# Shared-kernel convolution with per-pixel selection: one block of constants, an earlier deviation, a shorter first selection and loads in another order

## The reference

```
logits = conv1x1(gn(x), coupler_w) + coupler_b
sel    = softmax(logits);  sel = sel / sel.sum()
conv   = conv3x3(gn(x), weight as 8*64 filters) + bias
out    = x + sum_s conv[s] * sel[s]
```

## Time and profile before

| what | value |
|---|---|
| median of three runs | 340.92 us (340.84 to 341.65) |
| the profiled execution | 341.6 us, span 339.8 us |
| PE busy | 324.7 us, 96% of the span |
| DVE busy | 277.7 us, 82% |
| POOL busy | 229.5 us, 68% |
| ACT busy | 109.2 us, 32% |
| DMA | 41.93 MB, mean 123 GB/s |

### The profile page before, as it was taken

The page is one execution under the profiler, slowest core; times in us unless marked ns, Lnnn a source line. Parts: engine busy times, 40 slices in busy tenths (PEclk is TensorE's granted clock), DMA queues, the critical chain, the costliest instruction groups (busy, mean ns, idle before and its releaser), DMA issues.

```text
span 339.8 us, 5413 instructions
## 1 busy us (share of the span) xinstructions
PE 324.7 (96%) x1684; PEld 152.7 (45%) x1684; DVE 277.7 (82%) x504; ACT 109.2 (32%) x159; POOL 229.5 (68%) x329
## 2 busy tenths in 40 slices
PE   8996999999998999999999999999999899999993
PEld 8433444445443444445444444444544344444441
DVE  2799899997799688887799688887799687777786
ACT  1688251176111162175221062175221011111110
POOL 3700788899984598899854599899854599434343
PEclk9999899999999999999999999999999999999999
DMA  6799399019940695019950595019820596011002
GB/s 214 292 265 215 76 215 224 7 41 243 244 115 0 168 214 119 3 42 237 206 154 3 152 218 128 0 35 236 179 49 0 146 221 134 0 38 31 3 1 69
DMA packets 30374, 41.93 MB, mean 123 GB/s; under 512 B 2128, under 2 KB 23248, under 8 KB 29968
## 3 DMA queue, kind: packets, MB, share of 16 engines
q1 hardware_dynamic: 29184, 37.78, 46.0%
q10 hardware_dynamic: 1168, 3.89, 3.9%
HBM read 12.56 MB, written 4.72 MB: 51 GB/s over the span
## 4 chain that ended last, share of the span: by engine, by line
PE 69%; DVE 19%; issue 4%; DMA 4%; POOL 2%; SPq 1%; ACT 1%; DVEq 1%; ACTq 0%
PE pair L398 42%; PE pair L410 14%; PE pair L406 10%; DVE high L823 4%; DVE pair L822 3%; DVE half L831 3%; DVE pair L806 2%; DVE pair L808 2%; DMA op<-v_tail 2%; DMA x_raw<-x 2%; POOL v_pts L1112 2%; PE side L388 1%; DVE mix L790 0%; DVE v_pts L996 0%; DVE top L780 0%
## 5 line engine op out<-in xcount | busy, mean ns | idle before, releaser
L398 PE MATMUL pair<-w_head,op 128*128 128x512 f16 x864 | 234.9, 381 | 6.8 <-DVE half L831 3.5
L398 PEld LDWEIGHTS pair<-w_head,op 128*128 128x128 f16 x864 | 83.5, 98 | 110.6 <-DVE half L831 8.5
L410 PE MATMUL pair<-w_tail,op 128*128 128x512 f16 x288 | 109.4, 380 | 0.0
L594 ACT ACTIVATE m_sb<-pair 128x512 f32<-128x512 f32 x72 | 42.9, 596 | 200.6 <-PE pair L410 194.0
L1135 POOL TENSOR_TENSOR quarter<-half 128x256 f32<-128x256 f32 x71 | 52.8, 744 | 65.9 <-DVE half L831 65.3
L822 DVE TENSOR_TENSOR pair<-pair,sel_now 128x512 f32<-128x512 f32 x71 | 49.4, 696 | 38.9 <-PE pair L410 38.9
L831 DVE TENSOR_TENSOR half<-pair,high 128x512 f32<-128x512 f32 x71 | 49.1, 692 | 10.2 <-DVE high L823 1.0
L406 PE MATMUL pair<-w_tail,op_two 128*128 128x512 f16 x144 | 54.9, 381 | 0.0
L806 DVE TENSOR_TENSOR pair<-pair,m_sb 128x512 f32<-128x512 f32 x72 | 49.6, 689 | 0.0
L808 DVE TENSOR_TENSOR pair<-m_sb,pair 128x512 f32<-128x512 f32 x72 | 49.3, 684 | 0.0
L823 DVE TENSOR_TENSOR high<-pair,sel_now 128x512 f32<-128x512 f32 x71 | 48.3, 680 | 0.0
(11 more groups left out here) (110 smaller groups left out, 197.4 us busy)
## 6 DMA issues: line engine op xcount, KB each, us to landing
op<-v_head SPq DMA_DIRECT2D x14, 600.0 KB, 8.0
x_res<-x_pix SPq DMA_DIRECT2D x8, 576.0 KB, 6.5
op_two<-v_head SPq DMA_DIRECT2D x14, 300.0 KB, 9.0
op<-v_tail SPq DMA_DIRECT2D x14, 300.0 KB, 6.8
op<-v_head SPq DMA_DIRECT2D x14, 288.0 KB, 8.4
out<-y_out SPq DMA_DIRECT2D x7, 576.0 KB, 4.0
x_raw<-x ACTq DMA_DIRECT2D x3, 1152.0 KB, 9.2
w_raw<-weight SPq DMA_DIRECT2D x3, 768.0 KB, 8.8
```

What stands on the lines that cost most here:

```text
L398: nc.tensor.matmul(dst, op[b][:, 0, j, at + r * PW:at + r * PW + P], w_head[:, j, r, :], start=fresh and r == 0, stop=False, skip_group_ch ...
L410: return nc.tensor.matmul(dst, op[b][:, 1, j, at:at + P], w_tail[:, j, 0, :], start=False, stop=True, skip_group_check=True)
L594: act.activation(m1_sb[:, i % LOOK, :], pair[i % SETS_OF_BANKS][:, 0, :], ACT.Copy).then_inc(m1_copied, 1)
```

## The change

**Constants.** `mats`, `coupler_w` (zeros included), `coupler_b` and bias become one block that the host lays out, `consts`, with one transfer on SP's queue in the place of `mats`. ACT's four transfers, POOL's memset and two semaphores go.

**Deviation.** On POOL `inverse_deviation(0)` stands ahead of all three pieces of the last x part, where one piece stood ahead of it.

**Coupler.** The two heads of the coupler weights move from DVE to ACT (`coupler_heads`, behind `first_heads(3, 0)`); DVE keeps the two tails.

**Weight tails.** `second_point_tails` has two instructions for three.

**Selection.** `divide_again`, the sum and the scaling of the first 12 columns become `weights_soon`, one instruction that scales and divides together. `divide_again(0, 0)` and the sum (`sums_soon`) follow in round 0 behind `halve(0)`. POOL's bias steps wait for them (`prep`).

**Order.** On DVE `seed(0, 0)` goes ahead of `mixed_tails`, both `last_row_tail` follow it, and `seed(1, 0)` goes ahead of `add_up(0, 0)` in one piece. SP's `load_res(0, 0)` goes behind `first_fill(0, 1)`. ACT's `load_ahead(1)` goes behind `copy_m1(1, 0)`. `combine` goes from DVE's tile 4 to tile 3, in all rounds that prepare a next one.

```diff
+        consts = sb("consts", [P, 3 * P + 2 * SETS + SETS + C])
...
-            sp.dma_start(mats[:, :, :], matrices).then_inc(mats_loaded, 16)
+            sp.dma_start(consts[:, :], constants).then_inc(consts_loaded, 16)
...
             first_fill(0, 0)
-            load_res(0, 0)
             first_fill(1, 0)
             first_fill(0, 1)
+            load_res(0, 0)
             first_fill(1, 1)
...
+            def coupler_heads():
+
+                act.activation(cw_pts[:, 0, 1:3, :], cw_pair.unsqueeze(1).to_broadcast([P, 2, 2 * SETS]), ACT.Copy,
+                               scale=half_scale[:, 1:2]).then_inc(c_heads, 1)
+                act.activation(cw_pts[:, 0, 0, :], cw_pair, ACT.Copy, scale=minus_half_scale[:, 1:2]).then_inc(c_heads, 1)
...
-            act.dma_start(bias_all[:, :], bias.partition_broadcast(P)).then_inc(small_loaded, 16)
-            act.dma_start(cb_all[:, :], coupler_b.partition_broadcast(P)).then_inc(small_loaded, 16)
-            act.wait_ge(cleared, 1)
-            for b in range(2):
-                act.dma_start(cw_pair[C * b:C * b + C, b, :], coupler_w).then_inc(small_loaded, 16)
...
                 w_heads_of(0, slice(r, r + 1))
-            load_ahead(1)
             first_heads(3, 0)
+            coupler_heads()
             w_heads_of(1)
...
             copy_m1(1, 0)
+            load_ahead(1)
             first_heads(2, 1)
...
+            def weights_soon():
+
+                px = slice(0, SOON_PIX)
+                dve.wait_ge(prep, 14)
+                dve.scalar_tensor_tensor(sel_w[:, px, :], logit[:, px, :], undo[:, 0:1], spread(top[:, px], SETS),
+                                         ALU.mult, ALU.mult).then_inc(sel_copied, 1)
+
+            def sums_soon():
+
+                px = slice(0, SOON_PIX)
+                dve.wait_ge(prep, 15)
+                dve.tensor_reduce(sel_sum[:, px], mix[:, px, :], axis=AX.X, op=ALU.add).then_inc(prep, 1)
...
                     if begin and i == 0:
+                        divide_again(0, 0)
+                        sums_soon()
                         with_bias(0, 1)
                         maximum(0, 1)
...
-                    if more and i == 4:
+                    if more and i == 3:
                         combine(n + 1)
...
+                both = w_tail[:, :, :, :].rearrange("p k s n -> p (k s) n")[C:P, 2:6:3, :]
+                dve.scalar_tensor_tensor(both, w_pt2[C:P, 1:3, :], half_scale[C:P, 0:1], w_head[C:P, 1, 1:3, :],
+                                         ALU.mult, ALU.subtract).then_inc(w_tails, 2)
...
-            coupler_parts()
+            coupler_tails()
             input_tails_of(1, 1, 1)
             input_tails_of(0, 1, 2)
+            seed(0, 0)
             mixed_tails()
             last_row_tail(2)
-            seed(0, 0)
+            last_row_tail(3)
             with_bias(0, 0)
             maximum(0, 0)
             less_maximum(0, 0)
-            last_row_tail(3)
+            seed(1, 0)
             add_up(0, 0)
             invert(0, 0)
             divide(0, 0)
-            seed(1, 0, (0,))
             add_up_again(0, 0)
-            seed(1, 0, (1,))
             invert_again(0, 0)
-            divide_again(0, 0)
-            selection(0, sel_now_parts, sel_copied, 0)
+            weights_soon()
             round_(0, True, True)
...
+            inverse_deviation(0)
             pool.wait_ge(x_loaded[LOADS - 1], 16)
-            raw_point(1, LOADS - 1)
-            inverse_deviation(0)
-            for k in range(2, NP):
+            for k in range(1, NP):
                 raw_point(k, LOADS - 1)
```

More of the change, by code:

```diff
@@ L80, with program @@
 LOAD_AT = 14
-def program(nc, x, x_pix, weight, weight_mix, bias, coupler_w, coupler_b, matrices, out):
+def program(nc, x, x_pix, weight, weight_mix, constants, out):
     with ExitStack() as ctx:
@@ L110, in program @@
         ones_exp = sb("ones_exp", [1, 1])
-        cw_pair = sb("cw_pair", [P, 2, SETS])
         cw_pts = sb("cw_pts", [P, 2, 3, 2 * SETS], F16)
[L114 to L117, removed]
+        consts = sb("consts", [P, 3 * P + 2 * SETS + SETS + C])
+        mean_mat, diff_mat, eye_mat = (consts[:, k * P:(k + 1) * P] for k in range(3))
+        cw_pair = consts[:, 3 * P:3 * P + 2 * SETS]
+        cb_all = consts[:, 3 * P + 2 * SETS:3 * P + 3 * SETS]
+        bias_all = consts[:, 3 * P + 3 * SETS:3 * P + 3 * SETS + C]
         minus_half = sb("minus_half", [P, 1])
@@ L171, in program @@
         group_ps = side[:, PIX * SETS:PIX * SETS + 3]
-        mats_loaded = sem("mats_loaded")
-        small_loaded = sem("small_loaded")
+        consts_loaded = sem("consts_loaded")
         w_loaded = [sem(f"w_loaded{r}") for r in range(K)]
         ready = sem("ready")
-        cleared = sem("cleared")
         w_bounds = sem("w_bounds")
@@ L461, in _ @@
             warm_small(WARM_SMALL)
-            pe.wait_ge(mats_loaded, 16)
+            pe.wait_ge(consts_loaded, 16)
             group_sums(0)
@@ L744, in with_bias @@
                 dve.scalar_tensor_tensor(logit[:, px, :], logit_ps.rearrange("p (q s) -> p q s", s=SETS)[:, px, :], undo[:, 1:2],
-                                         cb_all[:, :].unsqueeze(1).to_broadcast([P, px.stop - px.start, SETS]),
+                                         cb_all.unsqueeze(1).to_broadcast([P, px.stop - px.start, SETS]),
                                          ALU.mult, ALU.add).then_inc(signal, 1)
@@ L953, in second_point_tails @@
                 dve.wait_ge(w_heads[1], 1)
-                for r, lo, hi, k, slot in ((0, 0, C, 1, 0), (1, C, P, 1, 0), (2, C, P, 2, 1)):
-                    dve.scalar_tensor_tensor(w_tail[lo:hi, k, slot, :], w_pt2[lo:hi, r, :], half_scale[lo:hi, 0:1],
-                                             w_head[lo:hi, 1, r, :], ALU.mult, ALU.subtract).then_inc(w_tails, 1)
+                dve.scalar_tensor_tensor(w_tail[0:C, 1, 0, :], w_pt2[0:C, 0, :], half_scale[0:C, 0:1], w_head[0:C, 1, 0, :],
+                                         ALU.mult, ALU.subtract).then_inc(w_tails, 1)
+                both = w_tail[:, :, :, :].rearrange("p k s n -> p (k s) n")[C:P, 2:6:3, :]
+                dve.scalar_tensor_tensor(both, w_pt2[C:P, 1:3, :], half_scale[C:P, 0:1], w_head[C:P, 1, 1:3, :],
+                                         ALU.mult, ALU.subtract).then_inc(w_tails, 2)
             def kernel_point2(r):
@@ L976, in last_row_tail, with coupler_tails @@
                                          w_head[0:C, k, 2, :], ALU.mult, ALU.subtract).then_inc(w_tails, 1)
[L978 to L985, removed]
+            def coupler_tails():
+                cw_two = cw_pair.unsqueeze(1).to_broadcast([P, 2, 2 * SETS])
+                dve.wait_ge(c_heads, 2)
                 dve.scalar_tensor_tensor(cw_pts[:, 1, 1:3, :], cw_two, half_scale[:, 1:2], cw_pts[:, 0, 1:3, :],
                                          ALU.mult, ALU.subtract)
-                dve.scalar_tensor_tensor(cw_pts[:, 1, 0, :], cw, minus_half_scale[:, 1:2], cw_pts[:, 0, 0, :],
+                dve.scalar_tensor_tensor(cw_pts[:, 1, 0, :], cw_pair, minus_half_scale[:, 1:2], cw_pts[:, 0, 0, :],
                                          ALU.mult, ALU.subtract).then_inc(c_tails, 1)
@@ L1035, in _ @@
             aggregate(0)
-            dve.wait_ge(small_loaded, 16 * 4)
-            dve.tensor_reduce(w_max[:, 1:2], cw_pair[:, :, :].rearrange("p b s -> p (b s)"), axis=AX.X, op=ALU.max,
+            dve.wait_ge(consts_loaded, 16)
+            dve.tensor_reduce(w_max[:, 1:2], cw_pair, axis=AX.X, op=ALU.max,
                               apply_absolute_value=True).then_inc(w_chain, 1)
@@ L1116, in input_and_bias @@
                 pool.wait_ge(sel_copied, n + 1)
+                pool.wait_ge(prep, PREP_CHAIN)
                 if 2 * (b * TPI + (j + 1) * BIAS_TILES) > SOON_PIX:
@@ L1122, in input_and_bias @@
                 pool.wait_ge(xb_done, done)
-                pool.tensor_tensor(bias_part[:, :, :], bias_all[:, :].unsqueeze(1).to_broadcast([P, q1 - q0, C]),
+                pool.tensor_tensor(bias_part[:, :, :], bias_all.unsqueeze(1).to_broadcast([P, q1 - q0, C]),
                                    spread(sel_sum[:, q0:q1], C), ALU.mult).then_inc(bias_done, 1)
@@ L1199, in _ @@
                 late_tails(k)
-            pool.wait_ge(small_loaded, 16 * 4)
+            pool.wait_ge(consts_loaded, 16)
             round_(0, True, True)
@@ L1222 @@
     matrices = np.stack([0.5 * same_group, eye - 0.5 * same_group, eye], axis=1)
+    coupler = np.zeros((P, 2 * SETS), np.float32)
+    for b in range(2):
+        coupler[C * b:C * b + C, SETS * b:SETS * b + SETS] = np.asarray(L0_conv_coupler_w).reshape(SETS, C).T
+    constants = np.concatenate([matrices.reshape(P, 3 * P), coupler,
+                                np.broadcast_to(np.asarray(L0_conv_coupler_b), (P, SETS)),
+                                np.broadcast_to(np.asarray(L0_conv_bias), (P, C))], axis=1)
     host = {
@@ L1228 @@
         "weight_mix": weight_mix,
```

(5 more changed lines are left out.)

1 line of the change is left out of this document (removed).

## The result

The changed kernel takes 341.96 us (median of 20 runs, 341.38 to 342.94). The kernel before, timed in turn with it, takes 341.52 us (20 runs, 340.82 to 342.69). The ratio is 1.0019, with a 95% interval of 1.001 to 1.0028: 0.3 to 1.0 us slower, within the 0.3% that was called no change. The forecast was +0.3 us. The profiled execution of after took 342.31 us with a span of 340.5 us, against 341.6 us and 339.8 us before: +0.7 us, a little more than the medians say.

What follows compares the result with a forecast made beforehand. DVE's work from 18 us to halve(4) was taken to bound the kernel: -1.60 us up to multiply(0), +2.21 us after, about +0.6 us at tile 7, -0.3 us elsewhere; +0.3 us, median 341.2 us, range 339.7 to 342.6 us.

Steps and rivals of the forecast that it cites:

- tile 7: PE's first points of tile 7 in round 0: about 0.6 us later than 55.76 us, between 55.5 and 57 us.
- end of round 0: PE's longest wait for halve: POOL gets halves earlier against PE, taken as -0.3 us (0 to -0.9).
- gap ahead of `multiply(0)`: DVE's wait for PE at 36.52 us goes as tails land earlier; saved 0.70 us (bounds 0.74 and 0).
- deviation, constants: At the start, POOL's earlier power saves 0.30 us (0 to 0.66); the constants cost nothing.
- coupler: On DVE before multiply(0), the two heads go to ACT, which waits there anyway; saved 0.42 us.
- selection and seeds: On DVE before multiply(0): selection saves 0.15 us; the earlier seed(0, 0) waits 0.15 us for ACT's copy.
- `divide_again`, sum behind `halve(0)`: Two instructions in DVE's gapless stretch: +0.55 us, plus +0.50 us for divide_again held by POOL (0 to 1.28).
- `less_maximum`: The DVE instruction at 42.48 us, held by POOL, now falls at POOL's next boundary: -0.20 us (0 to -0.30).
- `combine` ahead of `halve(4)`: Five DVE instructions now ahead of the event PE waits for in round 0: +1.36 us (bounds 0 and 1.36).
- The constants cost nothing.: Start: one transfer grows by 44 KB ahead of the weights, as much leaves ACT's queue; no cost.
- The rival that the start moves as a whole: If four small transfers hold x up, all to multiply(0) comes up to 1.5 us earlier; 339.7 us, chance 0.08.
- a held `combine` as a rival in rounds 1 and 2 alone: POOL holds combine another 0.85 us; PE waits 0.55 us in each of two rounds; 342.3 us, chance 0.12.

Runs made afterwards that it cites:

- loads back: The changed kernel with x_res and the next x loaded where they were before; 343.82 us, ratio 1.0067 to the kernel before.
- constants alone: The kernel before with only the block of constants added; 340.98 us, ratio 0.9977 to the kernel before.
- deviation back: The changed kernel with POOL's power back behind the first piece of the last x part; 341.77 us, ratio 1.0003 to the kernel before.
- selection undone: The changed kernel with divide_again and the whole first selection ahead of multiply(0) again; 342.71 us, ratio 1.0031 to the kernel before.
- tile 4: The changed kernel with combine back behind halve(4) of each round; 340.78 us, ratio 0.998 to the kernel before.
- not held: The changed kernel, combine at tile 3, its three steps with two SBUF operands written with per-partition scalars; 341.10 us, ratio 0.9982 to the kernel before.
- the four kernels that keep its start: Apparently the changed kernel with combine at tile 4 (340.78 us), combine's steps rewritten (341.10 us), loads back (343.82 us), selection undone (342.71 us).

## Why the forecast was right, point by point

The time was right (+0.44 us in the medians, +0.7 us in the profiled executions, +0.3 us forecast). Several of its terms were not: tile 7 came 1.0 us later than forecast, and the end of round 0 gave 0.6 us of that back. That the whole is as close as it is was luck in part. In us, minus is a gain:

| step | forecast | trace of after | shown by |
|---|---|---|---|
| gap ahead of `multiply(0)` | -0.70 | -0.70 | loads back: the gap returns, 0.77 |
| deviation, constants | -0.30, 0 | -0.08 together | constants alone -0.64; deviation +0.57 |
| weight tails | -0.18 | -0.13 | trace only |
| coupler | -0.42 | -0.41 | trace only |
| selection and seeds | 0.00 | -0.02 | selection undone: the selection alone saves 0.40 |
| `multiply(0)` | -1.60 | -1.34 | |
| `divide_again`, sum behind `halve(0)` | +1.05 | +0.84 | selection undone: 0.67 less to tile 7 |
| `less_maximum` | -0.20 | -0.12 | trace only |
| `combine` ahead of `halve(4)` | +1.36 | +2.26 | tile 4: 1.36; not held: 0.99 |
| tile 7 | +0.6 | +1.62 | |
| end of round 0 | -0.3 | -0.92 | wait 1.00 for 1.67 us, in part |
| whole | +0.3 | +0.7 | |

**What bounds the start.** Right: DVE's order of work decided, and the order of the loads was worth the gap ahead of `multiply(0)` (loads back: 0.74 us there). The last points of tile 0 start at 29.23 us at a granted clock of 1.00, and `multiply(0)` has no wait ahead of it, as the forecast said these would show.

**"The constants cost nothing."** This step failed: they gain. The rival that the start moves as a whole named the mechanism and counted against it that "they move under 50 KB"; x does land 2.6 us earlier. The gain by `magnitude` is only 0.64 us, because the warming matmuls then hold the group sums. The bytes were the wrong measure: with these few transfers on the second queue the engines stood half busy. Whether it is the queue or the small packets was not tried: of the transfers issued up to 21 us, 644 packets were under 512 bytes in before, and 208 with the block of constants alone.

**Deviation.** This step failed too. Its reason, the power behind a raw piece, was true of before, but the change's other part had already taken it away: with x early, the pieces are over and POOL is idle. I costed each part against the trace of before, and not against a start with the other part in it. What is left of the move is that three pieces come later, beside DVE's heads: +0.57 us.

**The two instructions behind `halve(0)`.** Right in kind and nearly in size: `divide_again` took 0.63 us instead of 0.26 us, held by a tail of POOL: 0.37 us more, where 0.50 us were forecast. With the loads back it took 1.18 us, 0.92 us more, inside the bounds of 0 to 1.28 us.

**`combine`.** The term of the sum that was mis-sized: 2.26 us for 1.36 us, outside its bounds of 0 and 1.36 us. I took the length at the old place for the new one; at the new place two of its steps meet two of POOL's instructions for their whole length. The forecast had a held `combine` as a rival in rounds 1 and 2 alone, and held against it that its 1.36 us "already hold a wait of that kind". In these rounds it lasts 1.33 us behind the second square and PE doesn't wait at tile 7, as forecast; the hold came in round 0. So one of the signs failed: first points of tile 7 start at 57.38 us and not between 55.5 and 57 us. (The working for rounds 1 and 2 adds up to 133.20 us, not 133.25 us; nothing hangs on that.)

**The end of round 0** took back 0.92 us and not 0.3 us. POOL's steps meet DVE's softmax there less: `less_maximum` takes 0.46 us for 1.13 us, `divide` 0.62 us for 1.10 us. These two make 1.15 us; that they are the cause of the shorter wait was read from the trace, not tried. The wait accounts for 0.67 of the 0.92 us; where the other 0.25 us go was not found.

## What to carry to other kernels

Cost the parts of a change one on top of the other: a wait that one part removes can't be gained again by the next, and moving work past it may then only push work into a worse place. A small instruction with two SBUF operands on DVE lasts here until POOL's instruction that is under way has ended, and its size says little; write it with a per-partition scalar where one operand is a column, before moving it. When a transfer or a wait is taken from the start, look at once for who is late next, here the warming matmuls.

## What the runs showed of the hardware

A few small transfers on a second queue cost much more than their bytes at the start: 0.55 of the DMA engines busy and 166 GB/s with them, 1.01 and 390 GB/s without them, in the same us. Which of their properties does it was not tried.

A `TENSOR_SCALAR` on a 128x1 column, with a per-partition scalar, is not held by POOL (0.20 to 0.27 us for each step), where the same subtraction as `TENSOR_TENSOR` took 0.84 us. That doesn't go for every `TENSOR_SCALAR`: `v_head`, on 128x576 elements, took 1.05 us in after with POOL's raw pieces beside it, and 0.51 us with the deviation back.

The granted clock is not the same in each execution behind the same wait. In the profile of after the wait of 2.02 us at 37.35 us left it at 1.00; in the one with `combine` at tile 4 the same wait of 2.02 us was followed by 0.50 from 38.2 to 41.6 us, and three matmuls took 1.19 us for 0.82 us. Four of the 20 runs of after had a mean clock of 0.991 to 0.992 and took 342.69 to 342.94 us; eleven at 0.999 to 1.0 took 341.38 to 341.97 us.

The granted clock doesn't tell all at the start either. Windows of after, columns as above:

```profile
4.00:5.00 1.00, 1.00 (x7) 1.00 (x6) 0.96 (x2) 0.00 (x0) 1.00 (x2) 1.00 1.03 402
...
7.00:8.00 1.00, 1.00 (x12) 1.00 (x11) 0.51 (x3) 0.00 (x0) 1.00 (x3) 1.00 0.97 362
```

Both show 1.00, yet PE gets through 7 of the same warming matmuls in one us and 12 in the other. When they speed up differs from execution to execution: the group copy of after and of the four kernels that keep its start came between 9.93 and 11.29 us. Intervals such as that from the group copy to `magnitude` (7.25 or 7.26 us in after and in the four kernels that keep its start) are therefore compared here, and not times from the span's start.
